# Orders of their own for the first and last steps of a four-layer graph kernel, and mask products of 64 rows

## The reference

```python
x = ln(x + L0(x, W, a, beta, adj))      # h = x W; e = leaky(s1_i + s2_j) * adj; elu(softmax(e) h + beta h)
x = ln(x + L1(x, adj, weight, bias))    # (adj x) W + bias
x = ln(x + L2(x, qkv, proj, ..., adj))  # 8 heads, -inf where adj == 0; o = attn proj + b; o + ln(o)*gamma + beta
x = ln(x + L3(x, adj, ...))             # three times: a = adj h
                                        #   z, r = sigmoid(...); hv = tanh(a w5 + (r h) u5); h = (1-z) h + z hv
```

## The kernel before, in words

| step i | begins at (its `l2_mask(i+1)`) | what it holds |
|---|---|---|
| -3, -2 | | layer 0 of units 0 and 1, layer 1 of unit 0, first half of layer 2 of unit 0 |
| -1 | 95.41 us | second half of layer 2 of unit 0; layer 1 of unit 1; layer 0 of unit 2 |
| 0 | 173.46 us | the first full step: layer 3 of unit 0 |
| 1 to 12 | 256.90 us, then every 83.4 us | full steps |
| 13, 14, 15 | 1258.17 us, 1339.04 us | no layer 0; then no layer 1; then layer 3 of unit 15 alone |

## Time and profile before

### The profile page before, as it was taken

One profiled execution on the slowest core, in us unless ns is written; L12 is line 12 of the kernel. 1 busy time (PEld: TensorE's weight loads), 2 busy tenths in 40 slices (PEclk: granted clock), 3 DMA queues, 4 the chain that ended last, 5 costly groups with the idle time before them and its releaser, 6 DMA issues.

```text
span 1485.5 us, 26652 instructions
## 1 busy us (share of the span) xinstructions
PE 1365.8 (92%) x10357; PEld 1153.5 (78%) x10357; DVE 1058.4 (71%) x2366; ACT 794.1 (53%) x1450; POOL 146.5 (10%) x196
## 2 busy tenths in 40 slices
PE   3566799999999999999999999999999999999885
PEld 2455688888888888888888888888888888878674
DVE  3455587777778787777778787777778787757444
ACT  1342455566656555565656555565656555555433
POOL 4300001110001011110001011110001001100000
PEclk8677799999999999999999999999999999999998
DMA  4000100000000000000000000001000000001000
GB/s 136 15 22 1 36 1 23 29 15 23 15 21 28 21 28 21 28 14 23 12 21 28 21 28 21 28 14 28 7 21 28 22 29 8 29 1 37 1 29 15
DMA packets 54661, 34.62 MB, mean 23 GB/s; under 512 B 34896, under 2 KB 51536, under 8 KB 54608
## 3 DMA queue, kind: packets, MB, share of 16 engines
q1 hardware_dynamic: 52800, 29.43, 6.7%
q0 software_dynamic: 1248, 3.94, 0.8%
q10 hardware_dynamic: 560, 0.52, 0.1%
HBM read 12.92 MB, written 8.39 MB: 14 GB/s over the span
## 4 chain that ended last, share of the span: by engine, by line
PE 67%; DVE 17%; ACT 8%; issue 4%; POOL 2%; DMA 0%; ACTq 0%; SPq 0%; POOLq 0%; DVEq 0%
PE banks L109 16%; PE banks L110 15%; PE banks L111 15%; PE banks L485 8%; PE banks L480 3%; PE banks L537 2%; PE banks L629 2%; ACT y L284 2%; PE banks L614 2%; PE banks L603 2%; DVE l_stats L256 2%; DVE l_r L1399 1%; ACT banks L982 1%; ACT l_qk L908 1%; DVE late_lo L1148 1%
## 5 line engine op out<-in xcount | busy, mean ns | idle before, releaser
L971 ACT ACTIVATE l_r<-banks,bias_r 128x512 f32<-128x512 f32 x96 | 65.9, 686 | 223.3 <-PE banks L111 223.3
L270 POOL TENSOR_TENSOR l_rstd<-l_mv,eps 128x4 f32<-128x4 f32 x48 | 28.3, 589 | 949.3 <-DVE l_mv L264 949.3
L988 ACT ACTIVATE banks<-banks,bias_h 128x512 f32<-128x512 f32 x96 | 63.3, 659 | 59.7 <-PE banks L111 59.6
L1148 DVE TENSOR_TENSOR l_rh_lo<-l_r,l_rh_hi 128x512 fp32r<-128x512 f32 x96 | 66.0, 688 | 36.6 <-ACT l_rh_hi L847 36.3
L1399 DVE SCALAR_TENSOR_TENSOR l_r<-banks,l_r 128x512 f32<-128x512 f32 x96 | 66.0, 687 | 32.1 <-ACT banks L982 29.2
L1381 DVE SCALAR_TENSOR_TENSOR l_r<-l_r,l_h 128x512 f32<-128x512 f32 x64 | 43.6, 682 | 55.4 <-ACT l_r L971 55.4
L284 ACT ACTIVATE y<-l_sum,l_offset,l_rstd 128x256 f32<-128x256 f32 x128 | 70.6, 591 | 19.0 <-DVE l_offset L278 19.0
L109 PE MATMUL banks<-l_rh_hi,u_hi 128*128 128x512 f32 x192 | 78.2, 408 | 0.0
L485 PE MATMUL banks<-adj_t,y 128*128 128x128 f32 x512 | 67.7, 282 | 10.9 <-ACT y L284 9.9
L982 ACT ACTIVATE banks<-banks,bias_z 128x512 f32<-128x512 f32 x96 | 63.5, 662 | 25.9 <-PE banks L111 25.9
L110 PE MATMUL banks<-l_rh_hi,u_lo 128*128 128x512 f32 x192 | 75.7, 394 | 0.0
(11 more groups left out here) (238 smaller groups left out, 4370.9 us busy)
## 6 DMA issues: line engine op xcount, KB each, us to landing
x_tok<-in_x_dram SPq DMA_DIRECT2D x16, 512.0 KB, 3.8
l_res<-y SPq DMA_DIRECT2D x16, 512.0 KB, 2.9
out_dram<-l_res SPq DMA_DIRECT2D x16, 512.0 KB, 2.9
l_vpair<-l_vstage SPq DMA_DIRECT2D x32, 128.0 KB, 3.1
w_raw<-in_L_gnn_w_w_dram POOLq DMA_DIRECT2D x3, 512.0 KB, 9.7
qkv_raw<-in_L_gnn_w_qkv_dram POOLq DMA_DIRECT2D x1, 768.0 KB, 7.4
u_raw<-in_L_gnn_u_w_dram POOLq DMA_DIRECT2D x2, 256.0 KB, 9.7
l_w_raw<-in_L_gnn_W_dram ACTq DMA_DIRECT2D x1, 256.0 KB, 4.8
```

Source lines behind the costliest of these rows:

```text
L971: nc.scalar.activation(b.r[:, m, :], RZ[:, m, :], ACT.Tanh, scale=0.5, bias=w.biases["r"][:, m:m + 1]).then_inc(s.r_ready.sem, 1)
L988: nc.scalar.activation(HV[:, m, :], HV[:, m, :], ACT.Tanh, bias=w.biases["h"][:, m:m + 1]).then_inc(s.hv_ready.sem, 1)
L1148: return nc.vector.tensor_tensor(parts[1][:, k, :], bank, parts[0][:, k, :].bitcast(F32), ALU.subtract)
```

## The change: what it does

`run` takes three functions now: `fill()` in place of the steps up to 0, `body(i)` unchanged in order for the loop, which runs over i = 1 to 11, and `drain()` in place of the steps 12 to 16. `fill` and `drain` are lists of their own on each of the five engines.

- In `fill`, units 0 and 1 go side by side: unit 0 uses `X` until its layer 3 (`front(u)`), unit 1 uses `Y`. Unit 1's `x` is loaded into layer 3's residual buffer at the start, and a few buffers of layer 3 are borrowed (`l1_parts`, `o_parts`). Layer 0 of unit 2 is woven into the second half of layer 2 of unit 0. All up to layer 3 of unit 0 is brought forward in this way; the work itself is the same.
- The start: `x` is transposed before the constants are done; DVE folds `a` into the weights first and makes the constants afterwards; the splits of weights are single pieces between the layers; PE transposes layer 3's weights into `Y` after layer 1 of unit 0.
- In `drain`, each layer of units 14 and 15 is brought forward, and layer 3 of unit 15 is woven with layer 3 of unit 14 from its step 1 on. For that unit 15 has semaphores (`TailSignal`), banks (`Y`) and buffers of its own (`own_of_last`: those of the early layers).
- `l2_mask` contracts over 64 rows, the two halves of the rows in turn, with two identities side by side as the stationary operand.
- `l2_scale` waits for `l2_x` where `l2_residual` did.

```diff
-FIRST, LOOP, LOOP_END, LAST = -4, 2, 12, 16
+LOOP, LOOP_END = 1, 12
...
-def run(eng, body, ahead_of):
-    for i in range(FIRST, LOOP):
-        if i in ahead_of:
-            ahead_of[i]()
-        body(i)
+def run(eng, fill, body, drain):
+    fill()
     with eng.Fori(LOOP, LOOP_END) as i:
         body(i)
-    for i in range(LOOP_END, LAST + 1):
-        body(i)
+    drain()
...
             for r in range(ROWS):
-                nc.tensor.matmul(Y[:, r, :], p.ident_bf[:, :],
-                                 p.mask_bias[:, :].unsqueeze(1).to_broadcast([P, TILES * CH, NODES]),
+                q = slice((r % 2) * NODES, (r % 2 + 1) * NODES)
+                nc.tensor.matmul(front(u)[:, r, :], p.ident2_bf[q, :, :].rearrange("p b j -> p (b j)"),
+                                 p.mask_bias[q, :].unsqueeze(1).to_broadcast([NODES, TILES * CH, NODES]),
                                  start=True, stop=False, skip_group_check=True)
```

More of the change, by code:

```diff
@@ L152, in _ @@
             sp.dma_start(p.adj2[q, :], p.a["adj"]).then_inc(loaded, 16)
[L154 to L180, removed]
+    return adj_blk, hits, count, zeroed, made, loaded
 GATES = ("u3", "w4s", "w5s", "diff", "u5")
@@ L357, in __init__ @@
[L357 to L361, removed]
+        self.adj_done, self.a_hi, self.a_lo = tail("l3_adj_done", between), tail("l3_a_hi", between), tail("l3_a_lo", between)
@@ L362, in __init__, with fused, is_first, is_second @@
+        self.tok_done, self.tok_ready = tail("l3_tok_done", each), tail("l3_tok_ready", between)
         self.l3_z, self.y3 = one("l3_z", 2), one("y3", 1)
-def fused(p, block, w, b, s, norms, src, dst):
+def fused(p, block, w, b, s, norms, src, dst, started):
     nc = p.nc
     X, Y = p.ps
-    RZ, HV = X[:, 0:2, :], X[:, 2:4, :]
     l0, l1, l2i, l2o, l3 = norms
     ws = w.sems
+    adj_blk, hits, count, zeroed, made, adj_loaded = started
+    def is_first(u):
+        return isinstance(u, int) and u == 0
+    def is_second(u):
+        return isinstance(u, int) and u == 1
+    def is_last(u):
+        return isinstance(u, int) and u == UNITS - 1
+    def front(u):
+        return X if is_first(u) else Y
+    def rz(u):
+        return (Y if is_last(u) else X)[:, 0:2, :]
+    def hv(u):
+        return (Y if is_last(u) else X)[:, 2:4, :]
+    def own(u):
+        return b.own_of_last if is_last(u) else b.own
+    def x_of(u):
+        return b.own.res if is_second(u) else b.x_tok
+    def l1_parts(u):
+        return b.f_hs if is_second(u) else b.late
+    def o_parts(u):
+        return b.f_as if is_first(u) else b.early
@@ L668, in gate, with a_parts @@
             return ins
-        def a_parts(step):
-            return b.l3_as if step else b.f_as
+        def a_parts(u, step):
+            return own(u).a_parts if step else b.f_as
         def wait_for_a(u, step):
@@ L1106, in _ @@
+        run(act, fill, body, drain)
     @block.vector
     def _(dve):
[L1108 to L1113 removed]
@@ L1372, in f_low_a, with h_before @@
             dve.wait_ge(*s.f_a_hi.at(u, k + 1))
-            lower(b.f_as, k, Y[:, 2 + k, :]).then_inc(s.f_a_lo.sem, 1)
-        def h_before(step):
-            return b.l3_h if step else b.f_h
+            lower(b.f_as, k, front(u)[:, 2 + k, :]).then_inc(s.f_a_lo.sem, 1)
+        def h_before(u, step):
+            return own(u).h if step else b.f_h
         @within
@@ L1546, in build @@
+        run(dve, fill, body, drain)
 def build(nc, a, out):
```

1899 lines of the change are left out of this document (1713 added, 186 removed).

## The result

| us | before | after |
|---|---|---|
| median (lowest, highest) of 4 runs each, taken together | 1489.01 (1486.86, 1492.82) | 1413.93 (1412.91, 1415.32) |
| the profiled execution | 1487.55 | 1413.15 |
| its span | 1485.5 | 1410.9 |

The ratio is 0.9494 with a 95% interval of 0.9471 to 0.9517. The forecast was 1417 us. I compare the traces by three marks, which are the same piece of work in both: the start of the mask of unit 2 (the loop begins), the start of the mask of unit 13 (the last written-out steps begin), and the end.

What follows compares the result with a forecast made beforehand. PE bounds the middle, while in the fill and drain handovers and waits leave it idle; fill 46.5 + drain 19 + mask 6.2 = 71.7 us off 1487.55 gives 1415.9 profiled, median forecast 1417 us, range 1398 to 1437.

Steps and rivals of the forecast that it cites:

- What bounds the kernel: Whole kernel: PE bounds the middle; in the fill no engine is full, a chain of handovers; drain PE 277.8 of 310.72 us.
- Part 1, start: Start of the fill: DVE begins when weights land, first product at about 12.5 us against 17.51, 5 us gained.
- Part 1, stages: Fill, unit 0 walked stage by stage to layer 3: l3_u(0,0,0) at 125 us against 176.00, 51 us earlier.
- Part 1, behind layer 3's start: Fill, from layer 3 of unit 0 to the loop: 80.9 us as before plus 2.5 half clock and 2 waits.
- the rival that the ends close better than walked: Fill and drain: added pieces fall into idle time, clock rises sooner, drain leaves 5 us; some 1400 us, chance 0.11.
- The rival of the queues: Fill: early waits in shared lists delay unit 0, 2.5 us more per six stages; 1439 us, up to 1450, chance 0.13.
- Part 2: Drain, units 14 and 15 woven: 28 us to be had, 9 stay, so 19 us gained, bounds 12 and 24.
- a few waits of 0.7 us, 1.5 together: Drain: short PE waits that the new list leaves, 1.5 us of the 9 us that stay.
- The wait at `l3_turn(14,0)`: Drain, unit 14: 2.2 us before the transpose, then f_turn(15) waits some 2 us for y2(15), with 1.5 us half clock.
- Part 3: l2_mask: 64-row products on different halves overlap, 0.44 us a unit, 14 units, 6.2 us gained, between 0 and 7.
- Part 4: Loop body and l2_scale's wait: order the same, a turn costs what the written-out step did; gain nothing.
- The rival "slower": Mask in every step: its new form stalls PE; with 5 us in place of 0.97 it would be 1491 us, chance 0.02.

Runs made afterwards that it cites:

- e3_turn_later: Changed kernel with the transposes of unit 1's x moved on PE from before unit 0's first products to behind l0_spread(0); 1408.35 us, ratio 0.9449.
- e4_x1_second: Changed kernel with unit 1's x loaded right behind unit 0's, ahead of the adjacency, PE's order unchanged; 1408.85 us, ratio 0.9452.
- e12_warm_drain: e10_turn_later_warm with 24 more idle transposes ahead of l3_turn(14,0) in the drain; 1404.46 us, ratio 0.9419.
- e1_mask128: Changed kernel with the mask products over 128 rows again, with a 128 x 128 identity; 1419.31 us, ratio 0.9519.
- e2_one_half: Changed kernel with all four 64-row mask products on the same half of the rows; 1422.28 us, ratio 0.9535.
- e9_warm: e8_both_starts with 84 idle transposes of the identity in four places of the fill where PE waits; 1407.38 us, ratio 0.9445.
- e8_both_starts: Changed kernel with the edits of both e3_turn_later and e4_x1_second; 1410.75 us, ratio 0.9467.
- e10_turn_later_warm: e3_turn_later with 84 idle transposes of the identity in four waits of the fill; 1405.16 us, ratio 0.9431.

## Why the prediction was right

The time, the mechanism and the order of the three parts held. That the sum came within 3 us is in part luck: against the forecast the stages of the fill gave 11.2 us more, its start 7.9 less, the part behind layer 3's start 4.5 more, and the drain with its masks 4.6 less. By its steps:

**What bounds the kernel.** Right. The gain lay in the ends, where no engine was full; one step of the loop still has 82.28 us of PE in 83.04.

**Part 1, start.** This is the sub-step that failed: "SP issues unit 1's `x` at once behind the adjacency (0.5 MB in the shadow of 8 us of loads)". I had read that DMAs issued by 2 us land by 8, and did not ask what a load issued at 3.86 finds in front of it. It landed at 18.8 us, PE's list puts its transposes ahead of unit 0's products, and the first product came at 20.45 in place of 12.5. e3_turn_later and e4_x1_second, which take away only that, gain 5.6 and 5.1 us. The 12.5 itself was right for an order without the wait (12.87).

**Part 1, stages.** I walked them too long: 28.4, 17.7, 18.7, 25.5 and 17.2 us were 25.9, 15.0, 17.1, 23.1 and 15.6. The sum of these five and the entry is 11.2 us less than walked, and the start took 7.9 back. Of the 8.5 us added for pieces of the neighbour unit, the 2 in the first stage fell into idle time (26.4 us before, 25.9 now), and of the 6.5 from the mask to layer 2's output 4.2 were spent (18.9 us before, 23.1 now). The other 6.3 of the 11.2 us lie in stages that I had put together from single lengths; no run says which piece was too long.

**Part 1, behind layer 3's start.** The 4.5 us for half clock and waits were not there: 80.80 us at clock 1.00, and PE busy 80.18 of them. Together 11.2 − 7.9 + 4.5 = 7.8 us, which is what the fill gained beyond 46.5. Of the rival that the ends close better than walked, the half about the fill came true and was partly hidden by the late load. The rival of the queues did not: no stage was longer than walked.

**Part 2.** 15.7 us, and the walk had 19, within its bounds of 12 and 24; with the old end the same kernel takes 312.7 us and not 295.0, some 2 us of it by the clock. What went into it: waits fell from 22.1 (the 20.9 of the earlier trace rows and 1.2 for `l_qk`) to 11.0, PE's busy time by 5.1, and the tail grew by 0.4: 11.1 + 5.1 − 0.4 = 15.8. The term that was mis-sized is "a few waits of 0.7 us, 1.5 together". They are eight kinds, 4.8 us: the scores and attention of layer 0 of unit 15 (0.9, 0.7, 0.7), the tokens of the new `h` (0.7), `l_qk` (0.6), `y` (0.5), two low parts (0.7). I take it that the old list hid most of these by the distance between its pieces, which bringing each layer forward shortened; no run tests that. The wait at `l3_turn(14,0)` was foreseen in size (2.2 and some 2 behind it, measured 3.96) and in place but for the order: it came whole ahead of the transposes, so `f_turn(15)` found its `y2` ready. The half clock behind it was put at 1.5 us; e12_warm_drain makes it 1.4 to 2.6.

**Part 3.** Right in mechanism and size: 0.42 us a step (0.44 forecast), 83.03 us a step, 0.54 us from mask to scores. Over the loop it is 4.6 us against the kernel before and 4.9 against e1_mask128, whose span is 6.2 us longer, with 1.5 of that in the fill. In the drain I had counted it and found nothing. The nearest row, the scores, led to the right one of two bounds. The Trainium skill (TensorEngine Tiling (Array Packing), Key Properties) says that a change of tiling mode drains the TensorE. If that cost a pause ahead of the mask, e2_one_half, which has the form of 64 rows and no overlap, would have a longer step than e1_mask128; it has 83.453 against 83.475 us. No run here shows such a cost of this second change of form.

**Part 4.** Right: the step is as long as before less the mask, and no wait for `l_x` shows.

**The rival "slower".** By its own terms (65.5 us gained, 16 masks at 5 us in place of 0.97) it comes to some 1489 us and not 1491. Nothing hangs on it: no mask took longer than before.

## What to carry to other kernels

- When a stage's first piece is brought forward, ask for its load too: when it is issued, how many bytes are then on the DMA engines, and what on the consumer's list stands behind its wait. Here moving two pieces behind the first unit's products was worth 5.6 us.
- Walk a chain that interleaves two units with stage lengths of the trace, and price an added piece by the stage it falls into. Here unit 1's layer 0 cost unit 0's nothing (25.9 us against 26.4), and layer 0 of unit 2 lengthened the stage from mask to output by 4.2 us.
- Two repairs of one wait don't add. Where an end of the program is a chain of short waits on PE, filling them with idle work can be worth more than it costs (3.1 to 3.4 us between medians here, with 1.1 of it in the drain, where nothing was edited, and 1.4 in the drain).
- Before a gain of a few us is read off two profiled executions, look at two kernels in which that stretch is the same. Here the same fill began the loop up to 3.1 us apart.

## What the runs showed of the hardware

- Two products of 64 rows that stand next to each other on different halves of the array overlap: four of them take 0.54 us from the first start to the next kind, against 0.96 us on one half, where 64 rows are no faster than 128. I had bounded this from both sides and taken it from the scores; the run shows it directly.
- Idle float transposes of 128 x 128 can keep the clock up: with them ahead of the entry of layer 3 the granted clock from 100 to 122 us is 1.00 in e9_warm to e12_warm_drain, and without them 0.92 in the changed kernel, e3_turn_later and e8_both_starts. From 20 to 50 us they do so in e10_turn_later_warm (1.00 throughout), and less in e12_warm_drain, which has the same fill (0.87, 0.96 and 0.83 for its three stretches of 10 us).
- The clock column does not show every half clock. In e3_turn_later it reads 1.00 from 12.87 to 19.43 us, while products of 258 columns start every 0.21 us, which is 258 columns at 1.2 GHz; in e4_x1_second they start every 0.12 us at the same reading. At the beginning of an execution the starts are to be read and not the column.

```profile
12.87:19.43 6.56, 5.53 (x24) 5.26 (x25) 5.52 (x16) 1.55 (x4) 3.25 (x4) 1.00 0.92 337
```

```profile
14.99:19.70 4.71, 3.68 (x27) 3.51 (x25) 3.82 (x14) 2.15 (x6) 1.12 (x1) 1.00 0.90 343
```
